# A two-stage residual block on one core: the sampling grid added by a matmul, batch norm operations moved, two weight products taken ahead, seven filling matmuls put in and three left out, and the last quantised product on whole integers

## The reference

```
# block 0, fp32
out = relu(group_norm(conv1x1(x, w1)))                # 256 -> 64 channels
om  = conv3x3(out, w_off) + b_off                     # 27 channels: 9 x offsets, 9 y offsets, 9 mask logits
out = sum_k w2[k] @ (bilinear_sample(out, grid_k + offset_k) * sigmoid(mask_k))
out = relu(group_norm(out))
x1  = relu(group_norm(conv1x1(out, w3)) + x)          # 64 -> 256
# block 1, activations to 16 bits, weights to powers of two
h = shift_conv(x1, w1)                                # 256 -> 64
h = relu(bn(shift_conv(h, peg_w, depthwise 3x3) + peg_b))
h = relu(bn(shift_conv(h, w2, 3x3)))
y = relu(bn(shift_conv(h, w3)) + x1)                  # 64 -> 256
```

## Time and profile before

| | us |
|---|---|
| median of 3 runs | 91.75 |
| lowest, highest run | 91.61, 92.53 |
| the profiled execution | 92.51 |
| its span, first to last instruction | 90.7 |
| PE busy, share of the span | 75.6, 83% |
| DVE busy | 65.4, 72% |
| ACT busy | 50.7, 56% |
| POOL busy | 5.0, 6% |

### The profile page before, as it was taken

The page is one execution under the profiler, slowest core; times in us unless marked ns, Lnnn a source line. Parts: engine busy times, 40 slices in busy tenths (PEclk is TensorE's granted clock), DMA queues, the critical chain, the costliest instruction groups (busy, mean ns, idle before and its releaser), DMA issues.

```text
span 90.7 us, 2168 instructions
## 1 busy us (share of the span) xinstructions
PE 75.6 (83%) x885; PEld 51.2 (56%) x885; DVE 65.4 (72%) x178; ACT 50.7 (56%) x91; POOL 5.0 (6%) x10
## 2 busy tenths in 40 slices
PE   4999999996899898999999998979579877776400
PEld 1325665565699797799896975443224474552100
DVE  1125449999999699996699617988884884848950
ACT  4101374779957999994874014509380254735760
POOL 7500110000000000000001300000000000000000
PEclk9999999999999999999999999999999999999995
DMA  2999800000000000000000000000000000000076
GB/s 27 311 322 316 335 3 0 0 7 0 0 7 0 0 7 0 4 11 0 0 7 0 0 0 7 0 0 0 0 0 0 0 0 0 0 11 0 0 248 215
DMA packets 3274, 4.17 MB, mean 46 GB/s; under 512 B 256, under 2 KB 2688, under 8 KB 3264
## 3 DMA queue, kind: packets, MB, share of 16 engines
q1 hardware_dynamic: 2992, 3.76, 12.8%
q10 hardware_dynamic: 272, 0.26, 0.8%
HBM read 2.98 MB, written 1.05 MB: 44 GB/s over the span
## 4 chain that ended last, share of the span: by engine, by line
PE 52%; DVE 29%; ACT 11%; issue 4%; DVEq 0%; ACTq 0%
PE acc L482 15%; PE slot L469 9%; DVE g_rows L893 8%; PE slot L361 6%; PE acc L609 5%; PE acc L372 3%; ACT g_cols L794 3%; PE slot L397 3%; PE acc L588 3%; ACT g_cols L707 2%; DVE g_cols L1039 2%; PE slot L546 2%; ACT pad L760 2%; DVE g_cols L992 2%; DVE stats L956 2%
## 5 line engine op out<-in xcount | busy, mean ns | idle before, releaser
L893 DVE TENSOR_TENSOR g_rows<-hats 128x2304 f32<-128x2304 f32 (+1 forms) x12 | 20.6, 1753 | 0.1
L707 ACT ACTIVATE g_cols<-slot 128x768 f32<-128x768 f32 x24 | 17.8, 830 | 3.7 <-PE slot L469 3.7
L482 PE MATMUL acc<-g_cols,v_sb 128*64 128x128 f32 x288 | 17.9, 276 | 0.0
L361 PE MATMUL slot<-zeros 128*128 128x512 bf16 x58 | 16.1, 412 | 1.2 <-DVE zeros L813 1.2
L482 PEld LDWEIGHTS acc<-g_cols,v_sb 128*64 128x64 f32 x288 | 15.5, 137 | 1.1 <-issue 0.3
L469 PE MATMUL slot<-consts_sb,g_rows 64*128 64x64 f32 x288 | 11.8, 226 | 2.1 <-DVE g_rows L893 1.7
L469 PEld LDWEIGHTS slot<-consts_sb,g_rows 64*128 64x128 f32 x288 | 10.3, 140 | 3.9 <-DVE g_rows L893 2.6
L361 PEld LDWEIGHTS slot<-zeros 128*128 128x128 bf16 x58 | 5.8, 108 | 8.0 <-issue 2.9
L760 ACT ACTIVATE pad<-g_cols 64x256 bf16<-64x256 int8 x8 | 3.3, 418 | 5.5 <-DVE g_cols L1039 5.4
L824 DVE BATCH_NORM_STATS2 stats<-acc 128x6 f32<-128x256 f32 x4 | 1.7, 430 | 5.1 <-PE acc L372 2.7
L397 PE MATMUL slot<-feat,woff_sb 128*64 128x256 f32 x36 | 4.7, 385 | 0.0
(11 more groups left out here) (140 smaller groups left out, 115.7 us busy)
## 6 DMA issues: line engine op xcount, KB each, us to landing
out<-g_cols SPq DMA_DIRECT2D x4, 256.0 KB, 2.3
x_sb<-x SPq DMA_DIRECT2D x3, 256.0 KB, 4.2
wq_sb<-wq SPq DMA_DIRECT2D x1, 484.5 KB, 5.9
woff_sb<-woff SPq DMA_DIRECT2D x1, 288.0 KB, 5.1
w_sb<-w SPq DMA_DIRECT2D x1, 288.0 KB, 5.2
x_sb<-x ACTq DMA_DIRECT2D x1, 256.0 KB, 3.3
w_sb<-w SPq DMA_DIRECT2D x1, 256.0 KB, 6.1
consts_sb<-consts SPq DMA_DIRECT2D x1, 232.0 KB, 5.1
```

What stands on the lines that cost most here:

```text
L361: nc.tensor.matmul(bank, zeros[:, 0:P], zeros[:], start=True, stop=True)
L482: mm = nc.tensor.matmul(acc[b2][rows(h), at:at + P], v_sb[:, B2 * h + b2, q, k, :], g_cols[t][h][:, NQ * k + q, :], start=(k == 0 and q == ...
L707: nc.scalar.activation(dst.rearrange("p k (r n) -> p k r n", r=HALVES), src.rearrange("p r (k n) -> p k r n", k=per), ACT.Copy).then_inc(g ...
L893: tt(g_rows[i % 3][:, taps], hats[:, t, h, 1, taps].unsqueeze(3).to_broadcast(shape), hats[:, t, h, 0, taps].unsqueeze(2).to_broadcast(sha ...
```

## The change

1. `IDLE[0]` is 6 instead of 7; `IDLE[15]` (2) is left out.
2. `grid_sb` has 128 partitions. The lower half holds the grid as before, the upper half is zeroed by VectorE. A matmul of `fold` with the grid joins the accumulation of the offset convolution, in the place of the tap that the upper half of the array lacked. ScalarE evacuates all 128 partitions in one operation with the bias (`copy_om`), and `add_grid` is gone. TensorE now waits for the grid and the constants before the first tap.
3. For images 1, the steps 2 to 4 of the offset convolution come behind the first two `make_v`, and ScalarE's evacuation comes behind the first two copies of v.
4. VectorE's six batch norm operations stand behind `pair_scale(3, 0)`.
5. Four fillers stand between turns 2 and 3, three between `sample(0, 0, 4)` and turn 6. The four are behind a wait for the eighth copy of v.
6. `w3q`, a fp32 product of 256 weight columns, is made behind `w1q`.
7. The last quantised product works on whole integers in fp32, 64 rows of the array per half of the batch. VectorE subtracts the constant for images 0, ScalarE for images 1. There are no bytes, no `n4`. The pieces come in the order of the images.

```
-PIECES = ((0, 0, 0, 2), (0, 1, 0, 2), (1, 0, 0, 2), (1, 1, 0, 2))
+PIECES = ((0, 0, 0, 2), (1, 0, 0, 2), (0, 1, 0, 2), (1, 1, 0, 2))
-IDLE = (7, 2, 3, 4, 8, 5, 1, 7, 7, 5, 0, 6, 0, 6, 0, 2, 0, 3)
+IDLE = (6, 2, 3, 4, 8, 5, 1, 7, 7, 5, 0, 6, 0, 6, 0, 2, 0, 3)

# TensorE, offset convolution
                     if k < TAPS:
                         mm = nc.tensor.matmul(slot[0][CB * p:CB * p + CB, BANK * b2:BANK * b2 + N],
                                               woff_sb[:, k, :], window(feat, b2, k), start=(s == 0),
-                                              stop=(k in (TAPS_A - 1, TAPS - 1)))
+                                              stop=(k == TAPS_A - 1))
+                    else:
+                        mm = nc.tensor.matmul(slot[0][CB * p:CB * p + CB, BANK * b2:BANK * b2 + N],
+                                              fold, grid_sb[:, N * b2:N * b2 + N], start=False, stop=True)
...
-            for b2 in range(B2):
-                pe.wait_ge(feat_ready, b2 + 1)
-                for s in range(TAPS_A):
-                    mm = om_step(b2, s)
-                    if b2 == 1 and s == 1:
-                        pe.wait_ge(consts_in, 16)
-                        om_turn(0)
-                mm.then_inc(om_done, 1)
+            pe.wait_ge(grid_in, 16)
+            pe.wait_ge(grid_zero, 1)
+            pe.wait_ge(consts_in, 16)
+            pe.wait_ge(feat_ready, 1)
+            for s in range(TAPS_A):
+                mm = om_step(0, s)
+            mm.then_inc(om_done, 1)
+            pe.wait_ge(feat_ready, 2)
+            om_step(1, 0)
+            om_step(1, 1)
+            om_turn(0)
...
-            for i in range(4):
-                make_v(i)
+            make_v(0)
+            make_v(1)
+            for s in range(2, TAPS_A):
+                mm = om_step(1, s)
+            mm.then_inc(om_done, 1)
+            make_v(2)
+            make_v(3)
             om_turn(1)

# TensorE, sampling
-            turns(0, 5)
+            turns(0, 2)
+            pe.wait_ge(v_ready, 2 * T)
+            idle(4, acc[1])
+            turns(3, 5)
             sample(0, 0, 4)
+            idle(3, acc[1])
             turns(6, 8)

# TensorE, first and last quantised product
-                if b2 == 1:
-                    idle(IDLE[15], spare)
...
-            for c in range(CH):
-                for b2 in range(B2):
-                    parts_ready(4, b2)
-                    nc.tensor.matmul(slot[c][:, BANK * b2:BANK * b2 + BANK], wqb[:, Q_W3 + P * c:Q_W3 + P * c + P],
-                                     flat(n4[:, b2]), start=True, stop=True).then_inc(qconv_done, 1)
+            for b2 in range(B2):
+                if b2 == 0:
+                    pe.wait_ge(whole_by_dve, 2)
+                else:
+                    pe.wait_ge(whole_by_act, CH * B2)
+                for c in range(CH):
+                    for h in range(HALVES):
+                        mm = nc.tensor.matmul(last_out(c, b2)[:, h, :], w3q[rows(h), P * c:P * c + P],
+                                              quot[:, 0, 0].rearrange("p b n -> p (b n)")[rows(h), N * b2:N * b2 + N],
+                                              start=True, stop=True)
+                    mm.then_inc(qconv_done, 1)

# ScalarE
-            def copy_om_rest(b2):
+            def copy_om(b2):
                 a.wait_ge(om_done, b2 + 1)
-                nc.scalar.activation(om_sb[CB:P, N * b2:N * b2 + N], slot[0][CB:P, BANK * b2:BANK * b2 + N],
-                                     ACT.Copy).then_inc(om_rest_ready, 1)
+                nc.scalar.activation(om_sb[:, N * b2:N * b2 + N], slot[0][:, BANK * b2:BANK * b2 + N],
+                                     ACT.Identity, bias=vec[:, V_BOFF:V_BOFF + 1]).then_inc(om_ready, 1)
...
-            copy_om_rest(1)
             for i in range(2 * T):
                 copy_v(i)
+                if i == 1:
+                    copy_om(1)
                 if i == 3:
                     copy_omt(1)
...
-            high_parts(4, lambda b2, h: n4[CB:P, b2, h, :])
+            a.wait_ge(quot_ready, CH * B2 + 3 * B2)
+            nc.scalar.activation(q2[:, N:2 * N], q2[:, N:2 * N], ACT.Identity, bias=minus_round[:, 0:1]
+                                 ).then_inc(whole_by_act, 1)

# VectorE (the six batch norm operations move as they are)
+            nc.vector.memset(grid_sb[CB:P], 0.0).then_inc(grid_zero, 1)
...
+            tt(w3q[:], wq_mag[:, Q_W3:Q_W3 + C], wq_sign[:, Q_W3:Q_W3 + C], ALU.mult).then_inc(wq_ready, 1)
...
                 quotients(0)
                 if n == 4:
-
+                    dve.wait_ge(quot_ready, CH * B2 + 2 * B2 + 1)
+                    ts(q2[:, 0:N], q2[:, 0:N], ROUND, None, ALU.subtract).then_inc(whole_by_dve, 1)
                     quotients(1)
-                    low_parts(0)
...
-                stt(flat(res[:, c, b2, h:h + n]), slot[c][:, at:at + N * n], bn_mul[:, 2 + c:3 + c],
-                    flat(y0[:, c, b2, h:h + n]), ALU.mult, ALU.add).then_inc(sum_ready, 1)
+                stt(res[:, c, b2], last_out(c, b2), bn_mul[:, 2 + c:3 + c],
+                    y0[:, c, b2], ALU.mult, ALU.add).then_inc(sum_ready, 1)
```

More of the change, by code:

```diff
@@ L140, in build @@
         woff_sb = sb("woff_sb", [P, TAPS, CB])
-        grid_sb = sb("grid_sb", [CB, PIX])
+        grid_sb = sb("grid_sb", [P, PIX])
         w2_sb = sb("w2_sb", [P, TAPS * CB])
@@ L149, in build @@
         w1q = sb("w1q", [P, CH * CB])
+        w3q = sb("w3q", [P, C])
         pegq = sb("pegq", [P, TAPS, CB], BF16)
@@ L213, in build @@
         slot = [ps(f"slot{i}", [P, 2 * BANK]) for i in range(3)]
-        acc = [ps(f"acc{b2}", [P, BANK]) for b2 in range(B2)]
+        both_acc = ps("acc", [P, B2 * BANK])
+        acc = [both_acc[:, BANK * b2:BANK * b2 + BANK] for b2 in range(B2)]
         small = [slot[2][:, BANK * b2:BANK * b2 + BANK] for b2 in range(B2)]
@@ L223, in build @@
         pads_zero = sem("pads_zero")
+        grid_zero = sem("grid_zero")
         bn_var_ready = sem("bn_var_ready")
@@ L308, in spread_of, with last_out @@
             return small[b2][:, P:2 * P]
+        def last_out(c, b2):
+            return ((slot[0], slot[1]), (both_acc, slot[2]))[b2][c][:].rearrange("p (h n) -> p h n", h=HALVES)[:, :, 0:N]
         def rows(h):
@@ L326, in _ @@
             sp.dma_start(woff_sb[:], woff).then_inc(woff_in, 16)
-            sp.dma_start(grid_sb[:], grid).then_inc(grid_in, 16)
+            sp.dma_start(grid_sb[0:CB], grid).then_inc(grid_in, 16)
             sp.dma_start(consts_sb[:], consts).then_inc(consts_in, 16)
@@ L566, in _ @@
             pe.wait_ge(std_ready, 4)
-            idle(IDLE[4], acc[0][:])
+            idle(IDLE[4], acc[0])
             conv3(1)
@@ L674, in distance @@
                 nc.scalar.activation(v, v, ACT.Relu, bias=one_sb[:, 0:1], scale=-1.0).then_inc(relu1_ready, 1)
-            v_banks = [small[0], small[1], acc[0][:], acc[1][:]]
+            v_banks = [small[0], small[1], acc[0], acc[1]]
             def copy_v(i):
@@ L682, in copy_v @@
                                      v_banks[i % 4], ACT.Copy).then_inc(v_ready, 1)
-            copy_om_rest(0)
+            copy_om(0)
             nc.scalar.preload_act_table(ACT.Sigmoid)
             make_mask(0)
-            copy_om_rest(1)
             for i in range(2 * T):
                 copy_v(i)
+                if i == 1:
+                    copy_om(1)
                 if i == 3:
@@ L777, in high_parts @@
                         src = byte(q2[rows(h), N * b2:N * b2 + N], 1, I8)
-                        high_part(dst(b2, h), image(src) if n < 4 else src, CH * B2 + B2 * (n - 2) + b2 + 1)
+                        high_part(dst(b2, h), image(src), CH * B2 + B2 * (n - 2) + b2 + 1)
             a.wait_ge(pads_zero, 3)
@@ L913, in _ @@
             make_hats(0)
-            add_grid(1)
             apply_mask(0)
@@ L942, in _ @@
             pair_scale(3, 0, V_GN2S, V_GN2B)
+            dve.wait_ge(bn_std_ready, 1)
+            settle(nc.vector.reciprocal(bn_std[:], bn_std[:]))
+            settle(tt(bn_inv[:], bn_std[:], vec[:, V_BNG:V_BNG + 4], ALU.mult))
+            settle(tt(bn_off[:], bn_inv[:], vec[:, V_BNM:V_BNM + 4], ALU.mult))
+            settle(tt(bn_off[:], vec[:, V_BNB:V_BNB + 4], bn_off[:], ALU.subtract))
+            settle(stt(bn_off[:, 0:1], bn_inv[:, 0:1], vec[:, V_PEGB:V_PEGB + 1], bn_off[:, 0:1], ALU.mult, ALU.add))
+            settle(ts(bn_minus[:], bn_off[:, 0:2], -1.0, None, ALU.mult))
             dve.wait_ge(wq_in, 16)
@@ L1088, in parts @@
                     quotients(1)
-                low_parts(1)
+                    low_parts(1)
             for b2 in range(B2):
@@ L1120, in _ @@
                 parts(n, [act[:, b2, :] for b2 in range(B2)],
-                      (lambda b2, h: inner(pads[1][0:CB, b2], h)) if n == 3 else (lambda b2, h: n4[0:CB, b2, h, :]))
+                      (lambda b2, h: inner(pads[1][0:CB, b2], h)))
                 if n == 3:
```

24 lines of the change are left out of this document (3 added, 21 removed).

## The result

The changed kernel takes 97.59 us (median of 4 executions, 96.99 to 98.79). The kernel before, run beside it on the same chip, takes 91.94 us (4 executions, 91.61 to 92.53). The ratio is 1.0568, 95% interval 1.0508 to 1.0628: slower by 5.7%. An execution more than 1.5% above the fastest of its kernel is left out of every ratio here, but not out of the medians. The prediction of 92.6 us, in a range of 91.2 to 93.2, is too low by 5 us.

A forecast was written before the change was run, and what follows sets the result against it. The chain runs through VectorE's hat products, then from 34.60 almost only TensorE, at full clock. Terms 0 + 0.75 + 1.05 - 0.51 - 0.41 = +0.88 us on the median 91.75 gave 92.6, range 91.2 to 93.2.

The forecast's parts named there:

- The front: Start to turns: VectorE 0.8 us ahead at the hat products, but ScalarE's copies of v release the turns; 0, -0.8 to +0.4.
- VectorE's lead arrives: Rival: at the turns, earlier copies of v start turn 2 up to 0.8 us sooner; 91.8 or 91.1 us; chance 0.12.
- Four fillers before turn 3: Among the turns: 0.96 us of fillers, with 0.87 caught up by three turns at ScalarE's pace; hidden within 0.1.
- Three fillers before turn 6: Before turn 6, where TensorE was itself last: no cover, so +0.75 us, bounds 0 and 0.8.
- The stall at the group means: Middle: 1.58 us more on VectorE against 0.55 of slack makes TensorE wait; +1.05 us, bounds 0.3 and 1.2.
- The clock: TensorE's clock, full in every slice but the last: no stretch behind the start could gain from a warmer one; no term.
- IDLE[15]: Two fillers less in the first quantised product, so its second half starts earlier; -0.51 us, between 0 and 0.54 saved.
- The last product: Tail, last quantised product on whole integers: first sum at 83.92 instead of 84.33; -0.41 us, bounds -0.6 and +0.4.
- (2): Sign in the front: ScalarE's copies of v still end near 22, and the four fillers are followed by turns without gaps.
- (6): Sign in the offset convolution: its 18 matmuls and 2 of the grid take the time of 18.
- (1): Sign in the middle: TensorE idle about 1 us before the group means near 52 to 53, ended by VectorE's moments.
- The one about the clock: Rival: before, the clock falls among the transposes in most executions and fillers prevent it; 2.4 us less, 90.2; chance 0.05.

The follow-up runs named there:

- experiment 4: The changed kernel with w3q and the six batch norm operations both moved behind the group moments; 92.80 us, ratio 1.0064.
- experiment 7: experiment 4 without the seven fillers among the turns; 91.79 us, ratio 0.9951.
- experiment 8: experiment 4 without the three fillers before turn 6, the four before turn 3 kept; 92.01 us, ratio 0.9955.
- experiment 2: The changed kernel with GpSimd's product starting only when all three weight products are done; 94.21 us, ratio 1.0180.
- experiment 3: The changed kernel with nine fillers on TensorE in front of the group means; 95.07 us, ratio 1.0287.
- experiment 6: The kernel before with the whole-integer last product, w3q behind the group moments and no IDLE[15]; 91.52 us, ratio 0.9922.
- experiment 5: The kernel before with only the six batch norm operations moved and w3q added as in the change, computed but not read; 96.77 us, ratio 1.0480.
- experiment 1: The changed kernel with w3q alone moved behind the group moments; 94.51 us, ratio 1.0123.

## Why the prediction was wrong

The order of events was forecast well and the price of one of them badly; the largest item, what follows from a long wait, was not in the sum at all. In the profiled execution:

- **The front, forecast 0 (-0.8 to +0.4): right.** The first hat product (L913) starts at 16.25 instead of 17.02, so VectorE has its lead of 0.8, and the copies of v still end at 21.27 + 0.67 = 21.94, only 0.10 sooner than the 22.04 of before: -0.10. The lead is lost there, as the text had it; the rival "VectorE's lead arrives" falls. One detail was priced wrongly and did no harm: the offset convolution waited 0.43 us for the constants, which land at 4.22 + 5.2 = 9.42 and not 9.3, with everything else ready earlier. (The zeroed half of the grid is the upper one, not the lower as the text says; its reasoning is the same.)

```profile
9.70 2.13 PE L402 MATMUL slot<-feat,woff_sb 128*64 128x256 f32 x17 [0.43 <-DMA consts_sb<-consts]
16.25 5.03 DVE L913 TENSOR_TENSOR g_rows<-hats 128x2304 f32<-128x2304 f32 x2
21.27 0.67 ACT L719 ACTIVATE v_sb<-slot 128x256 f32<-128x256 f32 x2
```

The bullets that follow use the timeline of after shown first.

- **Four fillers before turn 3, forecast hidden within 0.1: +0.28.** From the end of the copies of v to the first sampling products it is 25.08 - 21.94 = 3.14, where it was 24.90 - 22.04 = 2.86; with the -0.10 of the front that is the +0.18 at 25.08. The text let the catching up of three turns hide 0.96 us. But ScalarE's next three copies start when the first of them is done, and it had to wait 0.15 for it (the row at 24.21). Experiments 4, 7 and 8 say 0.27.
- **Three fillers before turn 6, forecast +0.75: measured +0.74** (0.92 - 0.18), and 0.74 between the profiles of experiments 4 and 8. It reaches turn 12 undiminished (+0.93).
- **The stall at the group means, forecast +1.05 (0.3 to 1.2): measured +2.09.** This is the step that failed first: "the product of 256 columns ... linear in the columns it is 0.42, of which 0.08 overlaps ...: 0.34". The interpolation is right for a product that runs alone: 0.33 in experiment 2. In after the step from w3q to the statistics is 1.32, because GpSimd's product starts 0.03 us sooner and w3q doesn't end until that one has. The other half of the term, the six operations at 1.24, came to 47.66 - 46.41 = 1.25. So 1.25 + 1.32 - 0.55 of slack = 2.02 of waiting, and 2.00 was seen. The row of w1q on which the interpolation was built gave no warning: in before GpSimd's product begins 0.12 before w1q ends (at 49.64), and behind w1q came statistics, which read PSUM and took their 0.75 beside it. But the place of the collision could be read there: GpSimd starts at 49.52, and what follows w1q on VectorE at 49.56.

```profile
49.52 1.15 POOL L352 TENSOR_TENSOR pegq<-consts_sb,wqb 128x576 bf16<-128x576 f32 x1 [37.20 <-DVE wqb L949]
```

- **The clock, forecast nothing behind the stall: measured +2.7.** The text says of the clock that "the trace has no stretch behind the start that a warmer clock could speed up", and never asks what a wait that the change adds could do to it. From 55.84 to 62.66 it is at 1.2 GHz. The sampling products and moments are 0.87 later by it (moments 57.87 instead of 53.98, +3.89 against +3.02). Then the eight fillers, which in before ended just as the feature map was ready, take longer than the wait that they cover, and the third convolution stands behind them: it is +5.73 late, 1.84 more. Experiment 3 takes all of this away by filling the wait: its third convolution starts at 60.35, 2.49 sooner, though its means come 0.22 later.
- **IDLE[15], forecast -0.51: measured -0.51.** The work is +5.73 late in front of this stage (62.84 against 57.11) and +5.22 behind it (the first product of the next stage starts at 78.25 instead of 73.03).
- **The last product, forecast -0.41: measured -0.37**, from +5.22 to +4.85. Experiment 6 has both parts at -0.9.

The sum as measured: -0.10 + 0.28 + 0.74 + 2.09 + 0.87 + 1.84 - 0.51 - 0.37 = +4.84, against 4.9 in the span. Of the points to look for, (2), (3), (4), (5) and (6) came out as forecast, and (1) with twice its length; for (6), from the convolution's first tap to ScalarE's copy it is 12.12 - 9.70 = 2.42, where it was 12.42 - 10.01 = 2.41. None of the rivals had a stall above 1.2 or a clock that falls behind it. The one about the clock looked at the wrong place, the transposes, since it started from the fillers in the change rather than from the waits.

**The lock.** The rows show one event in all nine kernels that make w3q: 1.40 with GpSimd's product started 0.03 or 0.04 before (after, experiments 3 and 5), 0.39 to 0.43 without it (experiments 1, 2, 4, 6, 7 and 8). The Trainium skill, "SBUF — State Buffer", section "Who interferes with whom", says that `tensor_tensor` "has no 2-port mode, but with both inputs in SBUF it **contends with GpSimd's reads**", and that the one that comes second waits for the whole instruction. The trace agrees: the weight product has both inputs in SBUF, comes second, and ends at 51.75 + 1.40 = 53.15, 0.28 after GpSimd's end at 52.87; the statistics with no input in SBUF pass beside the same GpSimd product (0.75 in experiment 1). By that rule and the 1.15 that GpSimd's product took in before, an estimate of the term would have been above 1.1 instead of 0.34.

**The clock gate.** The rows show that the clock fell after 2.0 us of idle TensorE in after and in experiment 5, and in one profiled execution after 1.03 (experiment 2). Two executions of experiment 1, with a stall of 0.70, had lower mean clocks (0.970 and 0.962), but no profile. On the other side no execution of experiments 3 and 4, 14 in all, without a wait there or with it filled, was below 0.983. A single execution proves little, though: 2 of the 33 of before, which has no such wait, show 0.966 and 0.968 as well, and 3 of the 20 of experiments 7 and 8 show 0.971. A mean clock is a rough witness too, since it also counts the fall behind TensorE's last instruction (the last digit of rows 1), which costs nothing. The Trainium skill, "TensorE: Matmul & The Clock Gate", Part 1, describes a clock that halves when the engine has had too little to do; that rule and the rows agree in kind. How much idle time is safe no run here settles: executions of one kernel with a wait of 0.70 or 1.03 us went both ways, and what the long ones met no row ties to the wait.

**What stays open.** The -0.51 and -0.37 were told apart in the trace of after only, not by a kernel for each. Experiment 7 is 0.27 us above experiment 6, within their intervals; it has the new front and the batch norm operations behind the moments, and whether either costs anything was not tried.

## What to carry to other kernels

When a change puts an instruction with two SBUF inputs on VectorE, look which GpSimd instruction is released at about the same time: here the product that released GpSimd stood two instructions ahead, and 0.4 us of work became 1.3. When a change adds a wait on TensorE, price the clock behind it too: here a wait of 2 us cost 2.5 us more through the clock, most of it because fillers sized for the full clock outlast their cover at half of it. And put setup work of no urgency behind the engine's next urgent result: the same seven instructions cost 4.2 to 4.8 us ahead of the group moments, and behind them no stall shows.

## What was not expected of the hardware

- A VectorE product of 256 fp32 columns with both inputs in SBUF took 1.40 us beside a GpSimd product of 1.15 us, and 0.39 to 0.43 without it; VectorE statistics from PSUM ran beside the same GpSimd product at their usual 0.75.
- TensorE idle for 2.00 and 2.02 us was followed by 6.8 us at 1.2 GHz, beginning 0.75 us after it had taken up work again in one kernel and 2.3 us after in the other (experiment 5). With stalls of 0.70 and 1.03 us the mean clock was lower in 2 of 4 and in 1 of 4 executions; that the stalls were the cause is not shown.
- Fillers are a fixed number of instructions, so at half the clock they double: eight of them 1.89 us at 2.4 GHz and up to 3.57 at 1.2.
